# Opening of the attention stages with heads of 16: a second spare bank, three scores ahead, row statistics in pieces

## The chip, the cores and the metric

One core of one Trainium2 chip runs the whole program. The metric is device time in microseconds (us), the median of three runs; lower is better. TensorE (PE) multiplies matrices into eight PSUM banks, VectorE (DVE) and ScalarE (ACT) empty those banks, GpSimd (POOL) does elementwise work and issues some transfers, and SyncE (SP) issues the others.

## What is computed

Four layers on x (4 batches x 512 rows x 256 columns, float32), each an attention and then a feed-forward network on normalised rows, both added to x. The attentions of layers 0, 1 and 3 have 16 heads of 16; layer 2 has heads of 32 and is not touched by what follows. Cut to the first layer that matters:

```python
q = (x @ Wq + bq).reshape(B, LQ, 16, 16).transpose(0, 2, 1, 3)      # layer 1
k = (ctx @ Wk + bk).reshape(B, LKV, 16, 16).transpose(0, 2, 1, 3)
v = (ctx @ Wv + bv).reshape(B, LKV, 16, 16).transpose(0, 2, 1, 3)
attn = softmax(einsum('bhqd,bhkd->bhqk', q, k) * 0.25)
x = x + (einsum('bhqk,bhkd->bhqd', attn, v) ... ) @ Wo + bo
```

Layer 0 does this twice for each batch with the same input: causal self-attention over x and cross-attention over ctx. Layer 3 is like layer 1 without biases. x is passed through a layer norm ahead of each attention.

## The kernel before

`attention` (L429) runs one attention stage. Its work is cut into **units**: eight heads of one batch of one job. Layer 0 has 16 units (4 batches, 2 jobs, 2 halves of the heads), layers 1 and 3 have 8. Unit 0 and unit 1 share a batch; in layers 1 and 3 unit 2 is the first of batch 1, in layer 0 it is the cross-attention of batch 0.

A unit needs, in this order:

- its k and its q, each projected on PE into one spare bank (L2021), copied twice by ACT into a full and a rounded half (L2474, L2475; the second copy frees the bank), split by POOL into the low half (L2643), written to DRAM by SP (L2752, L2753), and read back as a **stack** (L2762) in tiles named KS and QS;
- 16 **maxima steps** (4 pairs of heads x 4 query tiles): two matmuls into a double bank `bank_t` (L2092, in layer 0's causal job also mask matmuls, L2030), and one DVE reduction that empties it (L2281). After the last one DVE makes the row maxima (L2291, L2293), PE turns them (L2117), and they go through DRAM into QS (L2766, L2773);
- 16 **logits steps**: two matmuls into a `bank_t` (L2104) and one exponential on ACT that empties it (L2488);
- after every second logits step, eight matmuls of the probabilities with V into `bank_o` (L2134). V is projected once for each batch and job in two pieces (L2021 from Wv, emptied by L2271 on DVE, or in layer 3 by L2479 on ACT).

There are three `bank_t`, handed out in turn to maxima steps and logits steps, so each step waits until the step three before it in that row has been emptied. `misc` is a ring of spare banks for all other PE work. It holds one bank, `bank_m`: each projection, turn or V piece waits until the one before it has been copied out.

What sets the order is a small planner in `attention`. One **tick** is one logits step. `feed` hands out maxima steps up to a limit, at most two in a tick. `chores` is a list of other steps; in the main loop one of them is taken every second tick (gap 2). A step is put in every engine's program at the same place, and each engine runs its program in order.

The **opening** of a stage with heads of 16 is the code from L816 on: project unit 0 and unit 1 while the 16 maxima steps of unit 0 run; then `feed(lead, lead)`, which adds the first six maxima steps of unit 1 (`lead` is 22); then `begun` (layer 0 alone: turn the context with `load_context`, in four groups, and wait for the weights); then V of unit 0, `norm.rest`, k and q of unit 2, all before the first logits step. `norm.rest` is the layer norm's statistics of all batches that have none yet (L2209 and L2213, one instruction each for every tile of 128 rows) and, behind them, twelve small instructions for the inverse root (L2218 to L2232, called `root`). In layer 3 unit 2's k and q stand behind the normalising of batch 1 (L2239) and its turn (L2042, L2244, L2457), and so behind those statistics. Then the main loop begins.

## Time and profile before

| | |
|---|---|
| median of 3 runs | 3419.75 us (3411.82 to 3423.57) |
| the profiled execution's own time | 3418.18 us |
| its span, first to last instruction | 3416.4 us |
| mean granted TensorE clock | 0.887 of 2.4 GHz |
| busy | PE 2794.7 us (82%), DVE 1979.2 (58%), ACT 1440.9 (42%), POOL 1142.7 (33%) |

The stages run one after the other, with a wait of all engines for all others between them. Layer 0's attention begins at 0, layer 1's at about 660 us and layer 3's at about 2889 us. The rows below are the PE and DVE rows of these three openings. In a timeline row the bracket at the end is the idle time just before the row and what ended it.

### The profile page before, as it was taken

Reading aid. Unit: us, or ns where it says so; the run is one execution under the profiler, and the core shown is the slowest. Engines: PE = TensorE matmul, PEld = TensorE weight load, DVE = VectorE, ACT = ScalarE, POOL = GpSimd, SP = SyncE. Lnnn points to the kernel's source line nnn. Section 1 sums busy time; section 2 is a strip of 40 time slices with the busy share of each in tenths; the row PEclk is TensorE's granted clock in tenths of the full one; section 3 lists DMA queues with packets and bytes.
Section 4 is the critical chain, followed back from the end, with each engine's and each line's share of the span. In section 5 each row is a group of like instructions: output and inputs, shape, how many; then the busy total and the mean of one; then the engine's idle time right before and its main releaser. Section 6 shows DMA issues by size and latency. Waiting matters only on the chain. (4 is left out here: it accounts for less than half of the span.)

```text
span 3416.4 us, 45781 instructions
## 1 busy us (share of the span) xinstructions
PE 2794.7 (82%) x17261; PEld 1597.9 (47%) x17268; DVE 1979.2 (58%) x3631; ACT 1440.9 (42%) x1932; POOL 1142.7 (33%) x1030
## 2 busy tenths in 40 slices
PE   5898887778879789999867899778999998688544
PEld 2343433623336444445743344367777777233222
DVE  3655666577646364445747656664354443577588
ACT  1456556246622244545214455333333432266423
POOL 2233332213232246655315778640010110222333
PEclk7889997879969999999987999799999998699766
DMA  5666561155410001112100000001211221565100
GB/s 143 120 122 128 124 144 34 31 101 125 96 47 1 16 25 44 43 40 75 31 13 1 1 1 1 26 1 29 97 56 48 64 65 50 99 121 103 34 11 15
DMA packets 129740, 198.58 MB, mean 58 GB/s; under 512 B 36272, under 2 KB 66480, under 8 KB 129392
## 3 DMA queue, kind: packets, MB, share of 16 engines
q1 hardware_dynamic: 97776, 143.23, 18.5%
q0 software_dynamic: 31744, 52.41, 5.8%
q8 instruction: 138, 2.26, 0.3%
q14 instruction: 82, 0.67, 0.1%
HBM read 130.73 MB, written 64.75 MB: 57 GB/s over the span
## 5 line engine op out<-in xcount | busy, mean ns | idle before, releaser
L2281 DVE TENSOR_REDUCE L_mx<-bank_t 128x2 f32<-128x1024 f32 (+3 forms) x512 | 565.9, 1122 | 353.1 <-PE bank_t L2092 223.8
L2281 DVE TENSOR_REDUCE L2a_mx<-bank_t 128x2 f32<-128x1024 f32 x256 | 311.2, 1222 | 392.5 <-PE bank_t L2069 391.5
L2488 ACT ACTIVATE L_P<-bank_t 128x1024 f32<-128x1024 f32 (+3 forms) x384 | 340.0, 916 | 248.7 <-PE bank_t L2104 138.1
L2488 ACT ACTIVATE L2a_P<-bank_t 128x1024 f32<-128x1024 f32 x256 | 261.9, 1024 | 285.1 <-PE bank_t L2081 284.8
L2092 PE MATMUL bank_t<-L_KS,L_QS 48*128 48x512 f32 (+2 forms) x1024 | 242.6, 475 | 122.6 <-ACT L_P L2488 50.0
L2069 PE MATMUL bank_t<-L2a_QK 32*128 32x512 f32 x1536 | 252.9, 447 | 71.7 <-ACT L2a_P L2488 28.5
L2104 PE MATMUL bank_t<-L_QS,L_KS 50*128 50x512 f32 (+2 forms) x1024 | 243.2, 478 | 23.4 <-DMA L_QS<-L_spill_max_rows 12.6
L2077 PE MATMUL bank_t<-L2a_QK 32*128 32x512 f32 x1536 | 257.2, 443 | 0.0
L2069 PEld LDWEIGHTS bank_t<-L2a_QK 32*128 32x128 f32 x1536 | 136.9, 197 | 234.3 <-ACT L2a_P L2488 111.6
L2104 PEld LDWEIGHTS bank_t<-L_QS,L_KS 50*128 50x128 f32 x1024 | 100.5, 196 | 258.4 <-issue 170.8
L2134 PE MATMUL bank_o<-L_P,L_V 128*32 128x512 f32 (+3 forms) x1536 | 201.1, 599 | 8.2 <-ACT L_P L2488 7.0
L2021 PE MATMUL bank_t<-L2g_act_high,L2g_w_high 128*128 128x512 f32 x472 | 187.3, 397 | 19.3 <-DVE L2g_w_low L2365 17.0
L2092 PEld LDWEIGHTS bank_t<-L_KS,L_QS 48*128 48x128 f32 x1024 | 107.7, 207 | 199.5 <-ACT L_P L2488 85.8
L2643 POOL TENSOR_TENSOR L_lo<-L_full,L_hi 128x512 fp32r<-128x512 f32 x64 | 81.5, 1273 | 346.6 <-ACT L_hi L2475 317.4
L2372 DVE TENSOR_TENSOR L2g_act_low<-ctxT,L2g_act_high 128x512 fp32r<-128x512 f32 x96 | 67.4, 703 | 223.2 <-ACT L2g_act_high L2529 223.2
L2021 PE MATMUL bank_t<-L2g_act_low,L2g_w_high 128*128 128x512 f32 x472 | 185.3, 393 | 0.0
L2021 PE MATMUL bank_t<-L2g_act_high,L2g_w_low 128*128 128x512 f32 x472 | 185.0, 392 | 0.0
L2653 POOL TENSOR_TENSOR L2a_sums<-L2a_sums,L2a_P 128x1024 f32<-128x1024 f32 x64 | 153.3, 2396 | 18.3 <-ACT L2a_P L2488 14.0
L2648 POOL TENSOR_TENSOR L2a_diag<-L2a_P,after_q 128x256 f32<-128x256 f32 x128 | 95.2, 744 | 144.9 <-issue 80.0
L2134 PE MATMUL bank_o<-L2a_P,L2a_V 128*32 128x512 f32 (+3 forms) x896 | 138.8, 555 | 1.7 <-ACT L2a_P L2488 1.7
L2138 PE MATMUL bank_o<-L2a_P,ones 128*32 128x512 f32 x512 | 137.6, 614 | 0.0
L2077 PEld LDWEIGHTS bank_t<-L2a_QK 32*128 32x128 f32 x1536 | 130.1, 193 | 14.4 <-issue 11.3
(444 smaller groups left out, 6184.8 us busy)
## 6 DMA issues: line engine op xcount, KB each, us to landing
L_KS<-L_spill_k_halves SPq DMA_DIRECT2D x174, 128.0 KB, 5.3
L_QS<-L_spill_q_halves SPq DMA_DIRECT2D x174, 128.0 KB, 4.6
L_spill_raw<-xn POOLq DMA_DIRECT2D x64, 256.0 KB, 2.5
L2g_raw<-in_L_ffn_h_blocks SPq DMA_DIRECT2D x32, 512.0 KB, 3.8
L_spill_k_halves<-L_hi SPq DMA_DIRECT2D x32, 256.0 KB, 2.1
L_spill_k_halves<-L_lo SPq DMA_DIRECT2D x32, 256.0 KB, 2.4
L_spill_q_halves<-L_hi SPq DMA_DIRECT2D x32, 256.0 KB, 2.2
L_spill_q_halves<-L_lo SPq DMA_DIRECT2D x32, 256.0 KB, 2.8
```

The lines of the kernel that those rows point to most:

```text
L2021: mm = e.matmul(out_, w, x, start=first and i == 0, stop=last and i == len(terms) - 1)
L2069: mm = e.matmul(m.tile[:, c, :], Q[r, m.qt * P:(m.qt + 1) * P], K[r, :], start=i == 0, stop=i == 2)
L2077: e.matmul(l.tile[:, c, :], K[r, l.kt * P:(l.kt + 1) * P], Q[r, :], start=i == 0, stop=False)
L2092: mm = e.matmul(m.tile[:, c, 0:n_keys], st.QS[m.un.buf][rows, slot, m.qt * P:(m.qt + 1) * P], st.KS[m.un.buf][rows, slot, 0:n_keys], start ...
L2104: mm = e.matmul(x.tile[:, c, q0:S], st.KS[x.un.buf][rows, slot, x.kt * P:(x.kt + 1) * P], st.QS[x.un.buf][rows, slot, q0:S], start=True, s ...
L2134: mm = e.matmul(bank_o[row:row + 32, q0:q1], V[:, s.kt, head, :], moving, start=s.first and i == 0, stop=s.last and i == len(cuts) - 1, ti ...
L2138: mm = e.matmul(bank_o[row + 32:row + 64, :], ones[:, 0:32], s.at.Pr[pb][:, c, :], start=s.first, stop=s.last, tile_position=(0, row + 32))
L2281: e.tensor_reduce(neg, s.tile[:, :, 0:n_keys], AX.X, ALU.max, negate=True).then_inc(sem(s.done), 1)
L2488: e.activation(s.at.Pr[s.pb][:, :, q0:S], s.tile[:, :, q0:S], ACT.Exp, scale=s.at.scale).then_inc(sem(s.exp), 1)
L2643: e.tensor_tensor(s.low[:, :], s.full, s.high[:, :].bitcast(F32), ALU.subtract).then_inc(sem(s.lo), 1)
L2648: e.tensor_tensor(s.dst[:, :, :], s.src, after_q[:, :].unsqueeze(1).to_broadcast([P, 2, P]), ALU.mult).then_inc(sem(s.done), 1)
L2653: e.tensor_tensor(s.dst[:, :, :], s.a[:, :, :], s.b[:, :, :], ALU.add).then_inc(sem(s.done), 1)
```

## The change

The diff is in full. It does four things, all in stages with heads of 16 except that `norm.rest()` now returns a list:

- `misc` has two banks, `bank_m` and `bank_o`, until unit 0's V and unit 2's k and q are projected. Then `bank_o` is taken out of the ring and goes to the values.
- Ahead of that point three maxima steps of unit 1 are fed, not six. The rest is fed in the loop, two in a tick until the old distance is reached.
- `begun` becomes a chore behind unit 1's projections, among the maxima steps of unit 0.
- `norm.rest()` gives one chore for each batch and one for the root. These come after the main loop has begun, in front of the projections of unit 3 (units[1]'s V is an empty list here).

```diff
--- before.py
+++ after.py
@@ -350,8 +350,14 @@
                 self.e_stats[b:b + 1 if b1 is None else b1] = [e] * (1 if b1 is None else b1 - b)
 
             def rest(self):
-                if None in self.e_stats:
-                    self.stats(self.e_stats.index(None), B)
+                if None not in self.e_stats:
+                    return []
+                b0 = self.e_stats.index(None)
+
+                def roots():
+                    self.e_stats[b0:B] = [root(TB * b0, TB * B)] * (B - b0)
+                return [lambda b=b: rows_stats(lambda t: X[:, t, :], self.loaded, TB * b, TB * b + TB)
+                        for b in range(b0, B)] + [roots]
 
             def steps(self, b, ring, more=(), later=lambda n, step: step()):
                 if self.ready[b] is not None:
@@ -470,8 +476,8 @@
 
             tiles = Banks([bank_t[i] for i in range(3)])
             tiles.free = [[ALL.free[2 * i], ALL.free[2 * i + 1]] for i in range(3)]
-            o_free, misc = [ALL.free[6]], Banks([bank_m[:, :]])
-            misc.free = [ALL.free[7]]
+            o_free, misc = [ALL.free[6]], Banks([bank_m[:, :], bank_o[:, :]][:2 if D == 16 else 1])
+            misc.free = [ALL.free[7], ALL.free[6]][:2 if D == 16 else 1]
 
             units = []
             for b in range(B):
@@ -818,9 +824,11 @@
             if D == 16:
                 add(StackRest(st, st.ready, st.v_ones))
                 chores += prepare(units[1])
+                if begun is not None:
+                    chores.append(lambda: begun(misc))
             else:
                 if norm is not None:
-                    chores.append(norm.rest)
+                    chores += norm.rest()
                 chores += value_steps(units[0])
                 for un in units[1:st.n]:
                     chores += prepare(un)
@@ -829,15 +837,17 @@
                 add_fed(feed(unit_ticks))
                 run_due(gapped=False)
             run_all()
-            add_fed(feed(lead, lead))
             if D == 16:
-                if begun is not None:
-                    begun(misc)
-                chores += value_steps(units[0])
+                add_fed(feed(unit_ticks + 3, 3))
+                chores += value_steps(units[0]) + prepare(units[2])
+                run_all()
+                o_free[0] = misc.free.pop()
+                misc.aps.pop()
                 if norm is not None:
-                    chores.append(norm.rest)
-                chores += prepare(units[2]) + value_steps(units[1])
-                run_all()
+                    chores += norm.rest()
+                chores += value_steps(units[1])
+            else:
+                add_fed(feed(lead, lead))
             if side is not None:
                 side.ring, side.busy = misc, hi_free
                 chores += side.rest()
```

**PE, layer 0, from unit 1's maxima steps (out of KS, QS) to the first logits step (out of QS, KS).** Before:

```order
L2092 MATMUL bank_t<-L_KS,L_QS 128x128 x2
L2030 MATMUL bank_t<-L_mask_steps,L_mask_pick 128x64 x4
L2092 MATMUL bank_t<-L_KS,L_QS 128x256 x2
L2030 MATMUL bank_t<-L_mask_steps,L_mask_pick 128x64 x4
L2042 MATMUL bank_m<-ident,xn 128x128 x16
L2021 MATMUL bank_m<-L_Wv,XT 128x256 x8
L2021 MATMUL bank_m<-ctxT,L_Wck 128x512
L2021 MATMUL bank_m<-XT,L_Wcq 128x512 x2
L2092 MATMUL bank_t<-L_KS,L_QS 128x384 x2
L2030 MATMUL bank_t<-L_mask_steps,L_mask_pick 128x64 x4
L2104 MATMUL bank_t<-L_QS,L_KS 128x512 x2
```

With the change:

```order
L2102 MATMUL bank_t<-L_KS,L_QS 128x384 x2
L2040 MATMUL bank_t<-L_mask_steps,L_mask_pick 128x64 x4
L2031 MATMUL bank_o<-L_Wv,XT 128x256 x4
L2031 MATMUL bank_m<-L_Wv,XT 128x256 x4
L2031 MATMUL bank_o<-ctxT,L_Wck 128x512
L2031 MATMUL bank_m<-XT,L_Wcq 128x512 x2
L2102 MATMUL bank_t<-L_KS,L_QS 128x512 x2
L2040 MATMUL bank_t<-L_mask_steps,L_mask_pick 128x64 x4
L2102 MATMUL bank_t<-L_KS,L_QS 128x128 x2
L2040 MATMUL bank_t<-L_mask_steps,L_mask_pick 128x64 x4
L2114 MATMUL bank_t<-L_QS,L_KS 128x512 x2
```

The context's 16 turns are gone from here (they stand in four groups behind unit 0's sixth maxima step), three maxima steps have moved behind the projections of V, k (Wck) and q (Wcq), and two banks take turns. The line numbers of the change are ten higher.

**DVE, layer 1, from unit 1's first maxima steps on.** With the change:

```order
L2291 TENSOR_REDUCE L_mx<-bank_t 128x2 x3
L2281 TENSOR_TENSOR L_V<-bank_o,L_bv 128x32x16
L2281 TENSOR_TENSOR L_V<-bank_m,L_bv 128x32x16
L2291 TENSOR_REDUCE L_mx<-bank_t 128x2 x4
L2219 BN_STATS stats<-X 128x6 x4
L2223 BN_AGGR mv<-stats 128x2 x4
L2291 TENSOR_REDUCE L_mx<-bank_t 128x2 x3
L2219 BN_STATS stats<-X 128x6 x4
L2223 BN_AGGR mv<-stats 128x2 x4
L2291 TENSOR_REDUCE L_mx<-bank_t 128x2 x2
L2228 TENSOR_SCALAR nw<-mv 128x8
...
L2291 TENSOR_REDUCE L_mx<-bank_t 128x2 x4
```

Before, the same place reads:

```order
L2281 TENSOR_REDUCE L_mx<-bank_t 128x2 x6
L2271 TENSOR_TENSOR L_V<-bank_m,L_bv 128x32x16 x2
L2209 BN_STATS stats<-X 128x6 x8
L2213 BN_AGGR mv<-stats 128x2 x8
L2218 TENSOR_SCALAR nw<-mv 128x8
...
L2232 SCALAR_TENSOR_TENSOR rstd<-nw 128x8
L2281 TENSOR_REDUCE L_mx<-bank_t 128x2 x10
```

The eight tiles' statistics and the root stood between the V pieces and the loop's first reduction; now they stand in three pieces between the loop's first nine reductions.

**DVE, layer 3, the same place with the change, up to unit 2's normalised rows and their turn:**

```order
L2291 TENSOR_REDUCE L_mx<-bank_t 128x2 x3
L2219 BN_STATS stats<-X 128x6 x4
L2223 BN_AGGR mv<-stats 128x2 x4
L2228 TENSOR_SCALAR nw<-mv 128x4
...
L2242 SCALAR_TENSOR_TENSOR rstd<-nw 128x4
L2249 TENSOR_SCALAR xn<-X,mv,rstd 128x256 x4
L2254 COPY XT<-bank_m 128x512
L2291 TENSOR_REDUCE L_mx<-bank_t 128x2 x4
L2219 BN_STATS stats<-X 128x6 x4
L2223 BN_AGGR mv<-stats 128x2 x4
```

The statistics of four tiles stand ahead of the normalising, where twelve stood, and three reductions ahead of them, where six stood. Behind the first two units of each of the three stages the order is again the same on every engine.

## Rows read from the trace of the kernel before

**Rows 1.** Stretches of layer 0, busy us by engine; first line names the columns.
```profile
core 0: us, PE busy (x) PEld busy (x) DVE busy (x) ACT busy (x) POOL busy (x), PEclk, DMA share, GB/s
85.00:102.40 17.40, 16.31 (x107) 7.14 (x108) 6.57 (x13) 7.07 (x10) 2.54 (x2) 0.60 0.86 138
```

**Rows 2.** Timeline of PE, layer 0: start, duration, engine, line, tiles, count, idle before.
```profile
58.94 0.47 PE L2092 MATMUL bank_t<-L_KS,L_QS 48*128 48x128 f32 x2 [5.46 <-DMA L_QS<-L_spill_q_halves]
...
67.76 1.12 PE L2042 MATMUL bank_m<-ident,xn 128*128 128x128 f32 x4 [0.69 <-ACT ctxT L2457]
69.66 3.75 PE L2021 MATMUL bank_m<-L_Wv,XT 128*128 128x256 f32 x8 [0.78 <-ACT ctxT L2457]
74.39 3.78 PE L2021 MATMUL bank_m<-L_Wv,XT 128*128 128x256 f32 x8 [0.98 <-DVE L_V L2271]
78.95 1.13 PE L2021 MATMUL bank_m<-ctxT,L_Wck 128*128 128x512 f32 x2 [0.78 <-DVE L_V L2271]
81.59 3.45 PE L2021 MATMUL bank_m<-XT,L_Wcq 128*128 128x512 f32 x4 [1.51 <-ACT L_hi L2475]
84.97 0.62 PE L2092 MATMUL bank_t<-L_KS,L_QS 48*128 48x384 f32 x2
...
102.43 0.36 PE L2092 MATMUL bank_t<-L_KS,L_QS 48*128 48x256 f32 x2
```

**Rows 3.** Timeline of PE, layer 1.
```profile
662.80 3.38 PE L2021 MATMUL bank_m<-XT,L_Wq 128*128 128x512 f32 x4 [1.44 <-ACT L_hi L2475]
...
703.65 1.65 PE L2092 MATMUL bank_t<-L_KS,L_QS 48*128 48x512 f32 x6 [2.18 <-DMA L_QS<-L_spill_q_halves]
...
708.75 2.07 PE L2021 MATMUL bank_m<-L_Wv,ctxT 128*128 128x256 f32 x4
...
718.31 3.78 PE L2021 MATMUL bank_m<-XT,L_Wq 128*128 128x512 f32 x4 [1.36 <-ACT L_hi L2475]
722.02 0.80 PE L2092 MATMUL bank_t<-L_KS,L_QS 48*128 48x512 f32 x2
...
737.68 1.98 PE L2021 MATMUL bank_m<-XT,L_Wq 128*128 128x512 f32 x4
...
742.38 1.13 PE L2021 MATMUL bank_m<-L_Wv,ctxT 128*128 128x256 f32 x4 [0.37 <-ACT L_hi L2475]
```

**Rows 4.** Timeline of PE, layer 3.
```profile
2941.42 1.65 PE L2092 MATMUL bank_t<-L_KS,L_QS 48*128 48x512 f32 x6 [0.30 <-DMA L_QS<-L_spill_q_halves]
...
2957.93 1.11 PE L2042 MATMUL bank_m<-ident,xn 128*128 128x128 f32 x4 [6.58 <-DVE xn L2239]
...
2968.77 0.80 PE L2092 MATMUL bank_t<-L_KS,L_QS 48*128 48x512 f32 x2
```

**Rows 5.** Timeline of DVE, layers 0 and 1.
```profile
42.92 9.03 DVE L2281 TENSOR_REDUCE L_mx<-bank_t 128x2 f32<-128x256 f32 x12 [2.36 <-PE bank_t L2030]
...
704.49 6.88 DVE L2281 TENSOR_REDUCE L_mx<-bank_t 128x2 f32<-128x1024 f32 x6 [4.09 <-PE bank_t L2092]
...
714.74 2.70 DVE L2209 BATCH_NORM_STATS2 stats<-X 128x6 f32<-128x256 f32 x8
717.47 0.64 DVE L2213 BATCH_NORM_AGGREGATE mv<-stats 128x2 f32<-128x6 f32 x8
...
718.56 1.21 DVE L2223 TENSOR_SCALAR nw<-nw 128x8 f32<-128x8 f32 x1
...
735.03 1.23 DVE L2281 TENSOR_REDUCE L_mx<-bank_t 128x2 f32<-128x1024 f32 x1 [1.93 <-PE bank_t L2092]
```

**Rows 6.** Timeline of DVE, layer 3.
```profile
2953.09 0.91 DVE L2213 BATCH_NORM_AGGREGATE mv<-stats 128x2 f32<-128x6 f32 x12
...
2956.49 1.38 DVE L2239 TENSOR_SCALAR xn<-X,mv,rstd 128x256 f32<-128x256 f32 x4
...
2981.02 1.23 DVE L2281 TENSOR_REDUCE L_mx<-bank_t 128x2 f32<-128x1024 f32 x1 [1.15 <-PE bank_t L2092]
```

**Rows 7.** Timeline of POOL, layer 1.
```profile
718.47 1.27 POOL L2643 TENSOR_TENSOR L_lo<-L_full,L_hi 128x512 fp32r<-128x512 f32 x1 [30.34 <-ACT L_hi L2475]
```

## The prediction

> **What bounds the kernel now.** I read the table of stretches, then the PE and DVE timelines of the three openings of stages with heads of 16. "t" is a tick of the main loop, t0 its first; S is a maxima step.
>
> In the openings the bound is a chain of PE steps, each waiting until the one spare bank is emptied. Layer 0: PE waits 5.46 us for unit 1's stack until 58.94; then come six S, four turns of the context with 0.69 us of idle between them, two V pieces of 3.75 and 3.78 us, k and q (idle 0.78 to 1.51 us before each), and the loop begins at 84.97 [rows 2]. Layer 1 is the same without context: 703.65 to 722.02 [rows 3]. In layer 3 PE also waits 6.58 us for normalised rows that stand behind the statistics of twelve tiles: 2941.42 to 2968.77 [rows 4]. In the loop that follows PE is nearly full (16.31 of 17.40 us) and DVE is not (6.57) [rows 1]. So time saved ahead of the loop counts only as far as the loop's first ticks don't take it back.
>
> **The change, part by part.** Sum for each opening: when does the loop begin, and what do its first ticks cost.
>
> *Two banks ahead of the stack.* q no longer waits for k's copies. In layer 1 that wait is 1.44 us [rows 3], and q's spill, read and first S follow q; layer 3 is built alike. I let unit 1's stack land 1.4 us earlier in both: 702.2 and 2940.0. It can be nothing, if the reads are held by the transfer queue and not by their start; both ends stay in the range. In layer 0 I count nothing here (58.94).
>
> *Layer 0, to t0.* The turns of the context go among unit 0's S. There they cost four times 1.12 us of PE at most [rows 2] and delay the reductions; the slack is the 5.46 us for which PE waits for the stack anyway, so nothing is left on the path. From 58.94: three S 1.75 us (half the six, 3.4 us, rounded up), V 3.75 + 3.78 = 7.53 without a wait, k 1.13 to 2.08, q 3.45 to 3.78 [rows 2, 3] (k has half of q's matmuls, so the slow price of k is about half of 3.78 and a little over). t0 at 58.94 + 1.75 + 7.53 + 1.4 + 3.6 = 73.2, against 84.97: 11.8 us earlier.
>
> *Layer 1, to t0.* 702.2 + three S 1.65 + V 2 x 2.07 + k 2.0 + q 3.78 [rows 3] = 713.8. DVE is done with three reductions of 1.15 us (6.88 for six [rows 5]) and a V piece before k wants its bank. Against 722.02: 8.2 us.
>
> *Layer 3, to t0.* From 2940.0: 0.8 us to the first reduction, three reductions 3.45 us, four tiles' statistics 1.67 us (half of 2.70 + 0.64 [rows 5]), root 2.49 us (2954.00 to 2956.49 [rows 6]), normalising 1.38 us [rows 6]: 2949.8. Two turns of 1.11 us without a wait between, k 2.0, q 3.78 as in layer 1 [rows 3, 4]: 2957.8, against 2968.77: 11.0 us. The two V pieces fit in PE's wait.
>
> *The first ticks.* Here the change pays back. Three S and all statistics now stand between the loop's first reductions. Layers 1 and 3: up to the end of the reduction of t6's S, DVE has ten reductions (11.5 us), two statistics pieces (3.34 us) and a root (2.49 us); with 0.8 us until the first can start and some 0.9 us of waits that is 19.0 us, and DVE is what PE waits for through the `bank_t`. Before, it was 735.03 + 1.23 - 722.02 = 14.2 us in layer 1 and 2981.02 + 1.23 - 2968.77 = 13.5 us in layer 3 [rows 3 to 6]. So 4.8 and 5.5 us are given back, and k of unit 3, which moves from t4 to t6, runs in PE's waits. Net: 8.2 - 4.8 = 3.4 us and 11.0 - 5.5 = 5.5 us. Layer 0 has shorter causal reductions, 0.75 us (9.03 for twelve [rows 5]). Ten of them 7.5 us, three pieces 5.0, root 2.5: 15.0 us on DVE up to t7, and on PE about 12.6 us (16.31 us of [rows 1] less 3.78 and 2.08 for q and k makes 10.5 for 14 steps and the values; three more steps, 2 us). So about 15 us, then k and q of unit 3, which before stood inside, 3.1 to 5.9 us. Together 19.7 us against 102.43 - 84.97 = 17.5 [rows 2]: 2.3 us given back. Net 9.5 us.
>
> *Clock of TensorE.* All V, k and q pieces here but one ran at the 1.2 GHz level: 3.78 us for q where the same shape took 1.98 at 2.4 GHz, 2.07 for V where it took 1.13 [rows 3]. In layer 0 the level rose right behind the V piece that ran 74.39 to 78.17 (k then took 1.13 us) and was low again for q after 1.51 us of idle [rows 2]. With two banks these pieces run without a gap, so it may rise earlier. If it does: 3.4 us of V in layer 0, 1.8 us for q in layers 1 and 3, 7.0 us in all. If not: 0. I take 2.0, nearer to nothing, since layer 1's q at 718.31 was slow although V and k had run just before it.
> The Trainium skill, "TensorE: Matmul & The Clock Gate", section Part 1, says that the low level is the default and sustained activity releases it. By that rule the 7.0 us would come in full, and the total would be 25.4 us; the trace agrees for the one case in layer 0, and layer 1's q, behind 1.36 us of idle, neither shows nor excludes it.
>
> *Stalls of DVE beside POOL.* One root step took 1.21 us, where twelve of them took 2.49 in layer 3 [rows 6], while POOL's 1.27 us split ran from 718.47 [rows 5, 7]. Such a stall was beside PE work until now; in the loop it would be on the path. 0 to 1.0 us for each opening, 3 in all; I take 0, since one root in three met it.
> The Trainium skill, "SBUF — State Buffer", section "SBUF: two separate sides", says that the two engines share a port pair held by one instruction at a time, the loser being blocked fully. By it each root that meets a split pays that 1.0 us; this rule speaks against moving the root into the loop. The row agrees.
>
> **Sum.** 9.5 + 3.4 + 5.5 + 2.0 = 20.4 us. The profiled execution took 3418.18 us, 1.6 under the median of the three: 3397.8.
>
> **Rivals.**
> *A, as summed:* 3397.8; with its own bounds (stack no earlier -2.8, stalls -3, layer 0's k and q at the low level -1.5; clock up to +5.0) 3392 to 3406.
> *B, the first ticks take nearly all back.* DVE and PE wait for each other in turn: two S in one tick need two `bank_t` of three, and each piece of statistics then holds PE twice. If what is left in layers 1 and 3 (3.4 + 5.5 us) is lost outright, the clock gives nothing and layer 0 keeps 6 us, the gain is 6: 3412. For it: DVE's load is above PE's in those ticks. Against: only six or seven ticks long, and the PE work moved there fills the waits.
> *C, the clock rises in each opening* and stays up in the first ticks: 18.4 + 7.0, and some 1.3 us more in each loop: 29 us, 3389. For it: [rows 2] at 78.95. Against: [rows 3] at 718.31.
> *D, slower: the clock is lost.* PE waits for DVE in the first ticks, falls to 1.2 GHz and stays there. Price: a tick with values costs about 0.5 us more at that level (q alone 1.8 more). It decides from 40 such ticks on; if units 0 and 1 of all three stages (96 ticks) ran so, +48 - 20: 3446; 60 ticks: 3428. Against it: at 737.68 the level is high again about nine ticks into layer 1's loop although the ticks before it had waits.
> *E, no gain ahead of the loop:* unit 1's stack or maxima rows land later than PE is ready, because the context's turns delay unit 0's maxima in layer 0: 3.4 + 5.5 are left, without a gain by the clock: 3409.
>
> **Chances.** A 0.54, B 0.19, C 0.16, D 0.05, E 0.06. The range takes in C and B's nearer part: 3387 to 3411. A difference under 0.3% (10.3 us, from 3409.5) can't be told from none by this measurement. Faster than that: A, C and half of E and a little of B, 0.76; within: most of B, rest of E, 0.19; slower: D, 0.05.
>
> **What would show it.** In the trace after: q of unit 0 in layers 1 and 3 without a wait before it; the first logits about 11.8, 8.2 and 11 us sooner after the stage's start; in layer 3 the wait before the turn down from 6.58 to about 4 us. Then in the six ticks behind it PE waiting for DVE's reductions, DVE without gaps, and the tick t7 only 9.5, 3.4 and 5.5 us sooner. Wrong if the granted clock of the openings differs much, if PE still waits for a spare bank before k or q, or if anything behind the first two units of a stage changes its length by more than a few us.

## The result: 3382.48 us, 0.990 of before, and below the forecast's range

The changed kernel takes 3382.48 us (median of 6 runs, 3372.96 to 3397.53) against 3417.09 us for the kernel before (6 runs of the same comparison). The ratio is 0.990, 95% interval 0.9877 to 0.9922. The forecast was 3397.8 with a range from 3387 to 3411: the sign was right, the size was not. The profiled execution of the change took 3381.53 us, 36.6 less than the profiled execution of before, where 20.4 had been summed. Medians and ratios in this document are of undisturbed executions: one each of e5 and e12 and two of before, 4% to 83% longer than the rest, are left out.

The table of stretches of both kernels, each opening taken from a stage's first k projection to t0; before first, then the change (the first line names the columns):

```profile
core 0: us, PE busy (x) PEld busy (x) DVE busy (x) ACT busy (x) POOL busy (x), PEclk, DMA share, GB/s
13.97:84.97 71.00, 40.56 (x191) 21.87 (x191) 23.86 (x56) 9.31 (x15) 15.36 (x11) 0.64 0.52 118
660.27:722.02 61.75, 35.37 (x74) 13.47 (x75) 36.75 (x56) 6.92 (x11) 15.37 (x11) 0.57 0.48 94
2898.22:2968.77 70.55, 38.38 (x82) 14.86 (x82) 34.59 (x65) 8.71 (x14) 15.36 (x11) 0.55 0.40 83
```

```profile
14.10:70.45 56.35, 33.11 (x172) 18.73 (x173) 15.98 (x23) 9.09 (x15) 14.29 (x11) 0.73 0.67 142
648.69:696.80 48.11, 27.86 (x69) 11.81 (x70) 27.06 (x25) 6.91 (x11) 14.22 (x11) 0.65 0.59 111
2868.14:2924.65 56.51, 31.12 (x77) 14.01 (x78) 27.97 (x46) 8.71 (x14) 14.65 (x11) 0.63 0.47 95
```

The openings are 14.7, 13.6 and 14.0 us shorter; forecast were 11.8, 8.2 and 11.0. The granted clock in them is 0.63 to 0.73, where it was 0.55 to 0.64. Three maxima steps fewer stand ahead of t0, so a part must be given back.

PE of the change in layer 0, V, k and q of unit 2 and t0; the rows of before are [rows 2]:

```profile
61.80 3.78 PE L2031 MATMUL bank_o<-L_Wv,XT 128*128 128x256 f32 x8
65.38 2.38 PE L2031 MATMUL bank_m<-L_Wv,XT 128*128 128x256 f32 x8
67.59 1.02 PE L2031 MATMUL bank_o<-ctxT,L_Wck 128*128 128x512 f32 x2
68.54 1.98 PE L2031 MATMUL bank_m<-XT,L_Wcq 128*128 128x512 f32 x4
70.45 0.50 PE L2102 MATMUL bank_t<-L_KS,L_QS 48*128 48x512 f32 x2
```

PE in layer 1, from unit 0's q to the first ticks; before [rows 3]:

```profile
649.63 1.88 PE L2031 MATMUL bank_o<-XT,L_Wq 128*128 128x512 f32 x4
...
688.69 1.65 PE L2102 MATMUL bank_t<-L_KS,L_QS 48*128 48x512 f32 x6 [1.97 <-DMA L_QS<-L_spill_q_halves]
690.27 2.07 PE L2031 MATMUL bank_o<-L_Wv,ctxT 128*128 128x256 f32 x4
692.13 1.91 PE L2031 MATMUL bank_m<-L_Wv,ctxT 128*128 128x256 f32 x4
693.84 1.31 PE L2031 MATMUL bank_o<-ctxT,L_Wk 128*128 128x512 f32 x2
694.99 1.88 PE L2031 MATMUL bank_m<-XT,L_Wq 128*128 128x512 f32 x4
696.80 0.74 PE L2102 MATMUL bank_t<-L_KS,L_QS 48*128 48x512 f32 x4
...
698.63 0.50 PE L2102 MATMUL bank_t<-L_KS,L_QS 48*128 48x512 f32 x2 [0.86 <-DVE L_mx L2291]
...
704.85 0.79 PE L2102 MATMUL bank_t<-L_KS,L_QS 48*128 48x512 f32 x2 [1.61 <-DVE L_mx L2291]
```

From 688.69 to 696.80 the only bracket is the one in front of the first row: PE waits for nothing. V and k become shorter, and q takes 1.88 us where it took 3.78 (k, with half of q's matmuls, takes 1.31 where it took 2.08). In layer 3 PE waits 5.01 us for the normalised rows (6.58 before [rows 4]), and q takes 2.36:

```profile
2918.69 1.11 PE L2052 MATMUL bank_o<-ident,xn 128*128 128x128 f32 x4 [5.01 <-DVE xn L2249]
...
2922.36 2.36 PE L2031 MATMUL bank_m<-XT,L_Wq 128*128 128x512 f32 x4
2924.65 0.74 PE L2102 MATMUL bank_t<-L_KS,L_QS 48*128 48x512 f32 x4
```

DVE of the change in the first ticks of layer 1; before [rows 5]. It has hardly a gap from 697.35 until the root is done at 713.8, and PE waits for it (0.86 and 1.61 above):

```profile
697.35 4.62 DVE L2291 TENSOR_REDUCE L_mx<-bank_t 128x2 f32<-128x1024 f32 x4 [2.57 <-PE bank_t L2102]
701.88 1.40 DVE L2219 BATCH_NORM_STATS2 stats<-X 128x6 f32<-128x256 f32 x4
...
703.61 3.45 DVE L2291 TENSOR_REDUCE L_mx<-bank_t 128x2 f32<-128x1024 f32 x3
...
711.40 0.16 DVE L2228 TENSOR_SCALAR nw<-mv 128x8 f32<-128x8 f32 x1
...
713.70 2.35 DVE L2291 TENSOR_REDUCE L_mx<-bank_t 128x2 f32<-128x1024 f32 x2
```

### The profile page after: what moved, and what is told of

The parts are those of the page before. It is cut to its first block and busy times, and to the rows that moved or that the text cites. A ratio compares the mean times of both kernels' runs of the same rounds, so it can differ in the third digit from the quotient of the medians.

```text
span 3379.8 us, 45802 instructions
## 1 busy us (share of the span) xinstructions
PE 2767.3 (82%) x17268; PEld 1589.2 (47%) x17268; DVE 1978.0 (59%) x3643; ACT 1440.1 (43%) x1932; POOL 1143.1 (34%) x1030
## 5 line engine op out<-in xcount | busy, mean ns | idle before, releaser
L2114 PE MATMUL bank_t<-L_QS,L_KS 50*128 50x512 f32 (+2 forms) x1024 | 243.0, 478 | 21.4 <-DVE L_mx L2291 10.8
```

The costliest lines, as they stand in the source:

```text
L2114: mm = e.matmul(x.tile[:, c, q0:S], st.KS[x.un.buf][rows, slot, x.kt * P:(x.kt + 1) * P], st.QS[x.un.buf][rows, slot, q0:S], start=True, s ...
```

## The experiments

Two readings are taken from each trace, and stand in the table beside the median. **t0** is the start of the loop, counted in us from the stage's first k projection. **Kept** is what is left once the first ticks have given back their part: each ACT instruction is matched with the same one of the profiled kernel before, both are counted from the stage's first k, and the differences are averaged 130 to 160 us on in layers 1 and 3 and 200 to 300 us on in layer 0; a negative number is time saved. The second execution of before (e13) shows how far kept is to be trusted: within some 1.5 us in layers 0 and 3, and 4 us in layer 1. The three executions of the change differ by up to 3.6 us.

| kernel | median us | ratio (95% interval) | t0 in layers 0, 1, 3 | kept in layers 0, 1, 3 |
|---|---|---|---|---|
| before (profiled) | 3417.1 | | 71.0, 61.8, 70.6 | |
| change | 3382.5 | 0.9900 (0.9877 to 0.9922) | 56.4, 48.1, 56.5 | -15.0, -9.3, -8.6 |
| e8 change again | 3377.7 | 0.9910 (0.9888 to 0.9932) | 57.0, 46.5, 56.1 | -12.8, -8.0, -9.6 |
| e18 change, third time | 3383.1 | 0.9894 (0.9867 to 0.9921) | 55.8, 46.5, 56.5 | -15.6, -11.6, -9.1 |
| e13 before again | 3412.6 | 1.0006 (0.9989 to 1.0022) | 71.7, 59.8, 71.0 | +1.1, -4.0, +1.4 |
| e1 change, one bank | 3405.2 | 0.9979 (0.9956 to 1.0003) | 58.3, 58.5, 64.7 | -10.2, +3.8, -3.8 |
| e16 the same, waits filled | 3415.5 | 1.0001 (0.9980 to 1.0022) | 60.2, 55.4, 63.2 | -10.0, +1.7, -1.9 |
| e7 change, second bank late | 3392.6 | 0.9937 (0.9915 to 0.9960) | 58.3, 52.0, 60.1 | -13.6, -1.8, -9.1 |
| e5 before, second bank only | 3386.2 | 0.9938 (0.9910 to 0.9967) | 58.1, 49.8, 62.8 | -10.0, -11.1, -11.0 |
| e6 before, waits filled | 3416.0 | 1.0024 (1.0002 to 1.0047) | 69.6, 59.1, 68.6 | -6.6, +1.0, -6.5 |
| e3 change, statistics in front | 3384.6 | 0.9916 (0.9887 to 0.9945) | 56.9, 46.7, 59.1 | -6.0, -11.1, -10.2 |
| e11 before, statistics in pieces | 3414.4 | 0.9998 (0.9979 to 1.0018) | 72.1, 61.9, 67.8 | -4.4, +3.7, -4.0 |
| e4 change, context back | 3376.5 | 0.9893 (0.9867 to 0.9920) | 58.5, 46.6, 58.0 | -15.0, -10.8, -10.5 |
| e2 change, six ahead | 3373.7 | 0.9894 (0.9857 to 0.9932) | 56.3, 51.5, 59.1 | -21.3, -7.7, -10.9 |
| e9 change, six and context back | 3384.9 | 0.9914 (0.9880 to 0.9948) | 58.6, 50.4, 59.5 | -17.9, -10.4, -9.6 |
| e10 change, none ahead | 3372.1 | 0.9879 (0.9846 to 0.9912) | 50.6, 45.3, 49.6 | -17.8, -10.2, -14.2 |
| e17 the same again | 3373.4 | 0.9869 (0.9842 to 0.9897) | 49.4, 45.0, 48.9 | -14.9, -10.3, -13.7 |
| e14 none ahead, statistics behind k and q | 3373.4 | 0.9888 (0.9867 to 0.9908) | 50.1, 45.2, 48.6 | -16.5, -9.5, -14.1 |
| e12 change, idle work in a wait | 3374.5 | 0.9882 (0.9852 to 0.9912) | 52.8, 46.9, 55.6 | -19.6, -7.5, -13.3 |
| e15 e14 with idle work | 3377.4 | 0.9899 (0.9874 to 0.9924) | 52.2, 43.2, 50.2 | -12.1, -10.6, -16.8 |

Each ratio is against the runs of before in its own comparison (medians 3410 to 3417).

### The second bank

The change with one spare bank:

```diff
-            o_free, misc = [ALL.free[6]], Banks([bank_m[:, :], bank_o[:, :]][:2 if D == 16 else 1])
-            misc.free = [ALL.free[7], ALL.free[6]][:2 if D == 16 else 1]
+            o_free, misc = [ALL.free[6]], Banks([bank_m[:, :]])
+            misc.free = [ALL.free[7]]
...
-                o_free[0] = misc.free.pop()
-                misc.aps.pop()
```

> The changed kernel with one spare bank all the time; its other parts stay. Counted from a stage's first k projection, the loop begins 56.4, 48.1 and 56.5 us later with the change (layers 0, 1, 3). Theory 1, the second bank works through TensorE's clock: without it the waits of 0.8 to 1.5 us come back before each V piece, k and q, and the engine is at the low level again in them, so V, k and q of unit 2 take 3.8, 2.1 and 3.8 us in place of 1.9 to 2.4, about 1.3 and 1.9 to 2.4. Then the loop begins 6 to 8 us later in each opening and the kernel takes about 3382 + 20 = 3402. Rival, only the waits count: the same waits come back, 3 to 4 us an opening, but the pieces keep their lengths: 3393.

3405.2 us. PE in layer 1 of this kernel:

```profile
694.70 2.07 PE L2029 MATMUL bank_m<-L_Wv,ctxT 128*128 128x256 f32 x4
698.09 2.07 PE L2029 MATMUL bank_m<-L_Wv,ctxT 128*128 128x256 f32 x4 [1.32 <-DVE L_V L2279]
700.95 2.08 PE L2029 MATMUL bank_m<-ctxT,L_Wk 128*128 128x512 f32 x2 [0.79 <-DVE L_V L2279]
704.38 3.78 PE L2029 MATMUL bank_m<-XT,L_Wq 128*128 128x512 f32 x4 [1.35 <-ACT L_hi L2483]
708.09 1.22 PE L2100 MATMUL bank_t<-L_KS,L_QS 48*128 48x512 f32 x4
```

The waits are back, and with them the lengths of [rows 3]: theory 1 for layers 1 and 3 (10.4 and 8.1 us later). In layer 0 the loop begins only 1.9 us later, because k and q keep 1.12 and 1.98 us there although they wait: behind V pieces of 3.78 and 1.99 us the level stayed high across waits of 0.78 and 1.36 us. In the kernel before it did not (q 3.45 us behind a wait of 1.51 [rows 2]), so this is one case and not a rule. In layer 1 nothing of the gain is left, within the 4 us of that reading: with one bank, the other three parts show no gain there.

To part wait and level, the same kernel was given idle work in those waits (matmuls into `bank_o`, which nothing else uses then; their definition is left out):

```diff
-                chores += value_steps(units[0]) + prepare(units[2])
+                steps = prepare(units[2])
+                chores += filled(value_steps(units[0]), [0, 2]) + steps[:-2] + filled(steps[-2:], [2, 3])
```

> The changed kernel with one spare bank, and idle matmuls in TensorE's waits for that bank: two of 128x256 ahead of the second V piece and of unit 2's k, three ahead of its q. Theory 1 (of the 10.4 and 8.1 us by which one bank delays the loop in layers 1 and 3, the pieces' level is 3 to 4 us, the waits in them and in front the rest): q takes 1.98 in place of 3.78, the loop begins 2.5 to 4 us sooner than with one bank unfilled, at 54.5 to 56 and 61 to 62 us. Rival (the level is a small part): less than 1.5 us sooner.

PE in layer 1; the rows into bank_o are the idle work:

```profile
704.33 2.07 PE L2039 MATMUL bank_m<-L_Wv,ctxT 128*128 128x256 f32 x4
706.20 1.91 PE L2060 MATMUL bank_o<-XT,ident 128*128 128x256 f32 x4
707.90 1.60 PE L2039 MATMUL bank_m<-L_Wv,ctxT 128*128 128x256 f32 x4
709.34 1.03 PE L2060 MATMUL bank_o<-XT,ident 128*128 128x256 f32 x4
710.29 1.13 PE L2039 MATMUL bank_m<-ctxT,L_Wk 128*128 128x512 f32 x2
711.25 1.46 PE L2060 MATMUL bank_o<-XT,ident 128*128 128x256 f32 x6
712.77 1.98 PE L2039 MATMUL bank_m<-XT,L_Wq 128*128 128x512 f32 x4
```

The bank's waits are still there, filled, and k takes 1.13 and q 1.98 us. From the first V to t0 the granted clock reads (one bank, one bank filled, then the change):

```profile
694.70:708.09 13.39, 9.93 (x16) 4.01 (x15) 4.03 (x5) 1.26 (x2) 1.26 (x1) 0.50 0.11 40
704.33:714.68 10.35, 10.29 (x30) 6.59 (x28) 4.03 (x5) 1.27 (x2) 1.26 (x1) 0.77 0.00 0
690.27:696.80 6.53, 6.53 (x17) 3.77 (x16) 4.03 (x5) 1.26 (x2) 0.13 (x1) 0.68 0.01 3
```

So in this place it is work without gaps that brings the high level, not the bank as such. Layer 1 takes 13.4 us there with one bank, 10.4 with one bank filled and 6.5 with two: 3.0 us are the level's, 3.8 the waits'. In layer 3 the filling is worth 1.5 us, less than expected, and in layer 0, where the level was high already, it costs 0.7 from V to t0 (the other 1.3 us arose ahead of V). The median, though, is 3415.5, 10 us above the unfilled kernel's, and the two ratios' intervals overlap; kept is 2.1 us better in layer 1 and 1.9 worse in layer 3. So the level's part is shown at t0, and that it stays by itself is not. Nearly the same filling (one matmul less ahead of k) in the kernel before:

> The kernel before, one spare bank, with idle TensorE work added in its waits: two matmuls of 128x256 into the unused accumulator bank ahead of the second V piece, one ahead of unit 2's k, three ahead of its q. Nothing else changes. Theory 1 (the level follows from work without gaps): q of unit 2 takes 1.98 in place of 3.78 us in layers 1 and 3, V and k get shorter too, and the loop begins 1 to 3 us sooner in each opening although PE has more to do. Rival (it was the banks' handing on alone, and the level in these pieces is chance): q stays at 3.78, and the loop begins 0 to 1 us later.

q takes 1.98 us in all three openings, and the loop begins 1.4, 2.6 and 2.0 us sooner (2.2, 0.7 and 2.4 against e13). Theory 1 holds for the openings, and the kernel is still 0.2% slower (1.0002 to 1.0047). The traces show where, but not why. e6 kept 6.6 us in layer 0 and yet comes to layer 1's first k 4.7 us later than before; e16 kept 10.0 and is 1.2 ahead there, e1 kept 10.2 and is 10.8 ahead. Between 500 and 550 us, where the order of the instructions is the same again, the granted clock was 0.67 in e6 and 0.68 in e16, against 0.71 in e1 and 0.76 and 0.90 in the two executions of before. But e3, which has no idle work, shows it too (0.67, from 6.0 ahead to 1.6 behind), and the three executions of the change are 11.7, 21.7 and 16.3 us ahead at that k. That idle work is the cause is not shown.

The bank alone, added to the kernel before:

> The kernel before with the second spare bank alone: six maxima steps ahead of the loop, context and statistics where they were. Theory 1 (the bank is most of the gain, directly and through TensorE's clock): the loop begins 6 to 8 us sooner in layer 0, 9 to 10 in layer 1 (3.4 of it because q of unit 0 follows k at once and at the high level), 4 to 6 in layer 3, where the statistics still stand ahead; what is left 100 us on is 4, 9 and 3 us at least, the time about 3392 to 3396. Rival (the parts work only together, since with six steps ahead DVE is late and PE waits for it): less than 5 us in all, 3407.

3386.2: 21 us under before by the ratio (11 to 31 by its interval), where the change has 33; the loop begins 12.9, 12.0 and 7.8 us sooner, more than expected. The rival falls. By kept it holds 32.1 us in its three openings, as much as the change's 32.9: these traces don't show what the other three parts add, the medians alone do, within their spread. And the change with the bank given only for V, k and q of unit 2:

> The changed kernel with the second bank given only behind unit 1's first three maxima steps, for V, k and q of unit 2; units 0 and 1 are projected through one bank. Theory 1 (the front's gain is q of unit 0 behind k, 1.5 us of wait and 1.5 us of clock): unit 1's stack comes 3.4 us later in layer 1, 2.5 in layer 3 and about 0 in layer 0 than with the change, V, k and q keep their short times, and the kernel takes 3382 + 6 = 3388. Rival (stack and reads are held by the queue, the front gives nothing): the loop begins at the same place, 3382.

Unit 0's q takes 3.5 us again in layer 1, behind 1.4 us of wait, and the loop begins 3.9 us later than in the change (5.5 than in e8), in layer 3 3.6 and in layer 0 about 1.6. The median is 15 us above e8's and 10 above the change's: at least the 6 expected. The front is a part of its own.

### The other three parts

Statistics and root ahead of the loop again:

```diff
-                chores += value_steps(units[0]) + prepare(units[2])
+                chores += value_steps(units[0]) + (norm.rest() if norm is not None else []) + prepare(units[2])
```

> The changed kernel with the other batches' statistics and root ahead of unit 2's normalising again, that is ahead of the loop. Theory 1 (DVE's work is only moved, and DVE is what the first ticks wait for): layer 0 and 1 begin the loop at the same place and are within 1 us 100 us on; layer 3 begins it 3 to 4 us later (eight more tiles of statistics, 3.3 us, before the rows are normalised) and gets back most of it: 3384. Rival (statistics in the first ticks cost nothing, ahead of the loop everything): 3382 + 3.3 = 3386, and all 3.3 us of layer 3 stay.

Wrong in layer 0 by both theories. The loop begins at the same place, and then PE waits 5.65 us, since DVE works off twelve tiles' statistics and the root before it empties the `bank_t` of the steps at t0:

```profile
77.88 0.58 PE L2100 MATMUL bank_t<-L_KS,L_QS 48*128 48x256 f32 x2 [5.65 <-DVE L_mx L2289]
```

Kept in layer 0 is 6.0 us, against 12.8 to 15.6 with pieces. This is one trace, the slowest of four executions; the median, 3384.6, is not apart from the change's. In layers 1 and 3 the pieces are worth nothing (kept 11.1 and 10.2 us with statistics in front). In the kernel before the pieces alone bring nothing:

> The kernel before with the statistics in pieces behind the first logits steps alone: one spare bank, six ahead, context where it was. Theory 1 (TensorE waits for the bank and not for DVE as long as there is one bank, so the statistics lay beside that wait in layers 0 and 1; in layer 3 they stood ahead of the turn): the loop begins at the same place in layers 0 and 1 and 3 to 4 us sooner in layer 3, most of it given back: 3406 to 3410 against 3410. Rival (the 8.7 us that layer 0 lost with the statistics back in front are lost in the kernel before as well): 3400, layer 0 alone 7 to 9 us sooner 200 us on.

Theory 1 holds (0.9998); layer 0's 4.4 us are matched by a slower layer 1. By these traces the pieces pay only in layer 0 and only once the second bank has brought the loop forward.

The context behind unit 1's first maxima steps again, and the same with six ahead (`feed(lead, lead)`):

> The changed kernel with the four turns of the context behind unit 1's first three maxima steps again, as before the change; layer 0 alone. Theory 1: four times 1.12 us of TensorE at the low level come back between the maxima steps and V, with two banks hiding the copies, so layer 0's loop begins 4.5 us later; the clock has then risen by the V pieces (3.8 + 2.1), which gives 1 to 1.5 us back: +3 to +3.5, 3385. Rival: the turns' waits for their copies (0.7 us each) come back as well: +7, 3389.

> The changed kernel with six maxima steps of unit 1 ahead of the loop, as before the change, in place of three. Theory 1 (three steps moved into the loop cost there about what they save ahead of it in layers 1 and 3): the loop begins 1.7 to 3.5 us later in each opening, DVE's queue in the first ticks is 3.5 us shorter, and 100 us on nothing is left of the difference: 3382, within 3. Rival (the first ticks had room for the three steps): all of it stays, 3382 + 3 x 2.5 = 3390.

> The changed kernel with both six maxima steps ahead and the context behind them, so what is left of the change is the second bank and the statistics in pieces. Theory 1 (these two parts are the whole gain, the other two are worth less than 3 us each): 3376 to 3382, as the change, 0.990 of before. Rival A (each of the two undone parts was a loss, since the kernels without one of them took 3374 and 3376): their gains add, 3368 to 3372. Rival B (three ahead and the context among unit 0's steps do carry a part): 3386 or more, layer 0's loop beginning 6 us later and staying so.

Layer 0's loop begins 1.5 to 2.7 us later with the context back (e4 against the change's three executions), less than expected. With six ahead it begins 3.4 and 2.6 us later in layers 1 and 3, and nothing of that stays: kept is about the same in layers 1 and 3. In layer 0, where t0 does not move, it is larger (21.3, and 17.9 in e9, against 12.8 to 15.6), which these runs don't explain. The medians of the first two, 3376.5 and 3373.7, are not above the change's; both undone together give 3384.9. Their gains do not add (rival A falls), and 10 us between such medians can't be told from chance here. By e9, bank and pieces alone carry about 29 of the 33 us (18 to 41 by its interval).

None ahead (the line `add_fed(feed(unit_ticks + 3, 3))` taken out), twice:

> The changed kernel with none of unit 1's maxima steps ahead of the loop in place of three. Theory 1 (TensorE and DVE owe the same steps on either side of the loop's beginning): the loop begins 1.3 to 1.7 us sooner in each opening and all of it is given back in the first ticks, with 0 to 2 us more since DVE is what they wait for: 3382 to 3386. Rival (steps in the first ticks are free): 1.5 us more gain in each opening, 3377.

> The changed kernel with none of unit 1's maxima steps ahead of the loop, once more, beside the change in the same call. Theory 1 (what its openings hold more, 3 us in layer 0 and 5 to 6 in layer 3, is real, since in layer 3 the statistics, the normalising and the turn of unit 2 wait for three reductions less): 5 to 9 us below the change, 3372 to 3375, 200 us on again 3 us more in layer 0 and 5 us more in layer 3. Rival (its first time was a good draw): within 3 us of the change.

In layer 1 the loop begins 1.2 to 3.2 us sooner and nothing of it stays: given back in full, as theory 1 of the first run says. In layer 0 it begins some 6 us sooner; the 3 us more that the first run kept are not seen in the second. In layer 3 it begins 7 us sooner and 4 to 5 stay both times, which the first run's expectation missed. Here is PE in layer 3 of e17:

```profile
2917.72 0.66 PE L2051 MATMUL bank_o<-ident,xn 128*128 128x128 f32 x4 [1.10 <-DVE xn L2248]
...
2921.84 0.73 PE L2101 MATMUL bank_t<-L_KS,L_QS 48*128 48x512 f32 x4
```

The wait for the normalised rows is 1.10 us, where it was 5.01: the three reductions (3.49 us) stood ahead of the statistics on DVE. The medians are 3372.1 and 3373.4, and in the shared comparison 0.9869 against 0.9894 for the change (3383.1). The intervals overlap; that both medians lie some 10 us under the change's middle one speaks for none ahead, of which 4 to 5 us are seen in layer 3. No version had a lower median, but e2 and e14 (3373.7 and 3373.4) are not apart from it.

The remaining statistics right behind unit 2's projections, in layers 1 and 3, to empty DVE's queue for the first ticks (in layer 3 this kernel works out batch 1's statistics twice):

> The changed kernel with no maxima step of unit 1 ahead of the loop and, in layers 1 and 3, the remaining statistics and the root right behind the projections of unit 2 and ahead of the loop, where DVE would be idle; layer 0 keeps its pieces in the loop. Theory 1 (what the first ticks give back is DVE's queue): TensorE begins the loop at the same time as with none ahead (45.3 and 49.6 us), the first ticks have 5.8 us less DVE work in layer 1 and layer 3, and 2 to 4 us more are left in each: 3372 - 5 = 3367. Rival (the first ticks are bound by TensorE's own work, or DVE comes late to the first reduction): nothing gained, 3372 to 3376.

The rival: 3373.4. DVE then starts its first reduction only at 694.31 in layer 1, 4.4 us behind t0 at 689.91, and works through ten in a row. Moving DVE's work from one side of t0 to the other shifts the wait.

### Idle work in the long wait

> The changed kernel with 16 idle matmuls of 128x512 on TensorE while it waits for unit 0's stack (11 to 14 us of wait), into the next spare bank. Theory 1 (the level follows what TensorE has just done, so work in the wait keeps it high through unit 1's k and q): k of unit 1 takes about 1.1 in place of 2.07 us and q 1.98 in place of 2.2 to 3.8, its stack comes 1 to 3 us sooner in layers 1 and 3, the loop too: 3382 - 4 = 3378. Rival A (idle work costs its gain elsewhere, as where the gaps were filled): the openings gain that, the total does not move, 3382. Rival B (at the low level the 16 take 16 us and run past the stack's arrival): the loop begins 2 to 5 us later in each opening, 3392.

> The same with the 16 idle matmuls of 128x512 in TensorE's wait for unit 0's stack. Theory 1 (the level kept high through unit 1's k and q adds its 1 to 1.5 us in layers 0 and 1): 1 to 4 us below the kernel without them, 3364. Rival (in layers 1 and 3 they run past the stack's arrival by 2.8 to 3.4 us and take back what they give): the same time.

PE in layer 1 of e12, unit 1's k and q:

```profile
657.76 1.12 PE L2039 MATMUL bank_m<-ctxT,L_Wk 128*128 128x512 f32 x2
...
659.48 1.98 PE L2039 MATMUL bank_o<-XT,L_Wq 128*128 128x512 f32 x4
```

They took 2.07 and 2.5 to 3.8 us in the change. But the idle work runs past the arrival of unit 0's stack, taken from the change's trace, by 2.8 us in layer 1 and 3.4 in layer 3, so that t0 moves by 1.2 us at most there; in layer 0 it comes 3.0 to 4.2 us sooner. The medians, 3374.5 and 3377.4, are not apart from the same kernels without idle work.

### Both kernels again

> The changed kernel once more. Theory 1: what the openings gain is the same in each execution, within 1 us in each (the loop begins 56.4, 48.1 and 56.5 us behind the stage's first k), and the difference elsewhere, such as 10 us in the later part of layer 1, is the clock's and goes another way in another execution by some 5 us. Rival: the 10 us in layer 1's later part are a lasting effect of the change and are seen again.

> The kernel before once more, profiled. Theory 1 (its profiled execution of 3418 was a long one of its kind, and what all kernels seemed to gain 160 to 200 us into layer 1 was its loss alone): the new profiled execution takes 3405 to 3412, layer 1 comes out of the stretch 155 to 200 us behind its first k 3 to 4 us sooner, and the openings are the same within 1 us. Rival (the profile of before was typical): 3418 again, the same stretch as long as it was.

> The changed kernel a third time, as the other side of the comparison with none ahead. Theory 1: 3378 to 3383 and 0.990 to 0.991 of before, and the loop begins 56 to 57, 46.5 to 48.5 and 56 to 57 us behind the first k of layers 0, 1 and 3. Rival: 3372 to 3376, so that its first two medians were slow draws.

The openings repeat within 1.7 us at t0 for the change and 1.9 for before, not within 1: in layer 1 unit 1's q took 3.78 us in the first execution of the change and 2.5 in the other two. In that first execution PE works without a gap from 662.40, and the level is still low 8 us on, so unbroken work alone does not say when it rises:

```profile
662.40:670.49 8.09, 8.09 (x14) 2.67 (x14) 4.71 (x4) 1.26 (x2) 2.49 (x2) 0.50 1.04 171
```

The change's medians are 3382.5, 3377.7 and 3383.1, always 32 to 35 us under before. The new profiled execution of before took 3411.5 us, 6.7 less than the first, and differs most in layer 1: q of unit 0 took 1.98 in place of 3.38 us, and the stretch in which all kernels seemed to gain reads (first execution, then second):

```profile
809.00:821.00 12.00, 10.06 (x44) 4.45 (x42) 8.39 (x10) 5.27 (x6) 4.35 (x4) 0.72 0.87 129
```

```profile
809.00:821.00 12.00, 10.59 (x66) 4.60 (x63) 10.63 (x14) 7.34 (x9) 4.83 (x4) 1.00 0.88 132
```

At 0.72 of the clock the first does 44 matmuls, at 1.00 the second does 66. These 3 us belong to one execution of before and not to the change. The 10 us that the change gained beyond kept by 600 us into layer 1 came back as about 8 and 7 in its other two executions. The second execution of before is itself 5 to 6 us ahead of the first there, 3 of them in this stretch, so about half belongs to the first execution of before; the remainder is not explained by these runs.

## Why the forecast was wrong, step by step

The miss is 15.3 us. The openings kept 15.0 + 9.3 + 8.6 = 32.9 us against 20.4 summed, clock term included: 12.5. The profiled executions differ by another 3.7 elsewhere. That is a net figure: 3.3 are lost again in layer 0 behind kept, 9.2 more are gained between the first k of layer 1 and that of layer 3, some 3 of them in the stretch just shown, in which the execution that the sum started from was slow, and 2.1 are lost in layer 3. Against the second execution of before the openings kept 16.1, 5.3 and 10.0, in all 31.4, so the sum is firm and layer 1's share is not. The change's median lies 0.9 above its profiled execution, which takes that much off.

- **Two banks ahead of the stack, 1.4 us: too small.** Unit 1's stack is there 43.4 us behind the first k before (703.65) and 40.0 after (688.69), 3.4 sooner in layer 1 and 2.5 in layer 3. The wait of 1.44 was counted; that q behind k at once also runs at the high level (1.88 for 3.38 us) was not. e7 confirms it. In layer 0 the stack came 1.1 us later, where nothing was counted.
- **V, k and q up to t0, and the clock's 2.0 us: the step that failed.** From the first V to t0, 12.5 us were summed in layer 0 and 8.65 measured, 9.9 and 6.5 in layer 1, and from k on 5.8 and 4.2 in layer 3. That is 8.9 us for the three, and with the front's q 10 to 11, where 2.0 were taken and 7.0 were the upper bound. The 2.0 was chosen from layer 1's slow q at 718.31, which stood behind a wait; in e16 and e6, with the wait filled, the same q took 1.98. These lengths are measured up to t0; that they stay is shown only together with the waits' part (kept). Two rows of before spoke against reading the level from one piece and the wait in front of it: high behind 1.51 us of wait, low behind 0.20.

```profile
19.00 1.98 PE L2021 MATMUL bank_m<-XT,L_Wq 128*128 128x512 f32 x4 [1.51 <-ACT L_hi L2475]
...
681.56 3.78 PE L2021 MATMUL bank_m<-XT,L_Wq 128*128 128x512 f32 x4 [0.20 <-ACT L_hi L2475]
```

  The Trainium skill ("TensorE: Matmul & The Clock Gate", section Part 1) says that the low level is the default and activity releases it; by that rule the forecast had named 7.0 and 25.4 in all. The traces agree for unit 2's V, k and q (q 1.88 to 2.38 us in all three openings of all three executions), not for unit 1's q in layer 1, 3.78 us after 4.3 us of work without a gap. Rival C had the rise right and was still short; its high level did not last through the first ticks (the logits step at t0 took 0.40 us, the third 0.63).
- **Layer 3's chain on DVE: right.** 9.8 us from stack to normalised rows were summed, 9.9 measured; PE's wait is 5.01, near the 4 foretold.
- **The first ticks: right in layer 3, about right in layer 1, too high in layer 0.** Given back are 13.6 - 9.3 = 4.3 and 14.0 - 8.6 = 5.4 us, against 4.8 and 5.5. Against the second execution of before it is 6.4 and 4.4, so layer 1's agreement is in part luck. Layer 0 gives back nothing, against 2.3; why is open. Rival B falls.
- **Stalls of DVE beside POOL, taken at 0: right.** No root step in the change's openings took over 0.17 us. Where e14 put a root beside POOL's split, one took 1.24:

```profile
691.55 1.24 DVE L2237 TENSOR_TENSOR nw<-nw 128x8 f32<-128x8 f32 x1
```

```profile
691.50 1.26 POOL L2654 TENSOR_TENSOR L_lo<-L_full,L_hi 128x512 fp32r<-128x512 f32 x1 [0.43 <-ACT L_hi L2486]
```

  The first row is DVE, the second POOL of the same kernel. The price was right; among these rows it is paid only where the two meet.
- **The place of layer 0's statistics.** The forecast saw it only as a load moved onto the first ticks. e3 shows that in front it would have cost 5.65 us of wait: with the loop's beginning forward, the statistics no longer lie beside PE's wait for the bank.
- **Rival D** did not occur, and E neither. A's own bounds add up to 3393 to 3405 and not to 3392 to 3406; nothing rests on it.

## What to carry to other kernels

Where a chain of TensorE pieces waits for a bank between them, price the second bank twice: the waits, and the pieces behind them at the length of the high level, since both go together (3.8 and 3.0 us up to t0 in one opening here). When a start is brought forward, look again at what used to stand beside the old wait on the emptying engine; it is now on the path. Steps moved across the start of a loop are worth what the engine with the longer queue saves, which was nothing in layer 1 and 4 to 5 us in layer 3, where a chain stood behind them.

## What the runs showed of the hardware

- A wait of 1.35 to 1.44 us did not settle the level: q behind it took 1.98 us in the second execution of before (layer 1, unit 0) and 3.38 in the first, and in e1 3.78 behind layer 1's short V pieces against 1.98 behind layer 0's long ones. Nor did work without a gap: 8.09 us of it ran at 0.50 in layer 1 of the change.
- Idle work on TensorE raised the level wherever the pieces behind it had run low (q of unit 2 1.88 to 1.98 us in e6 and e16), and the whole program gained nothing from it (1.0024 and 1.0001 for two kernels whose openings began their loops sooner in two or three stages).
- POOL's split stretched the one root step that met it (1.24 us for 0.17, e14). Statistics beside such a split (689.78 to 691.06 in e14) kept 1.38 us for four, and the change's four reductions out of PSUM at 697.35 beside the split at 698.39 took 4.62, 1.15 each as elsewhere.
- The same program's profiled executions differ in single stretches by the granted clock, 0.72 against 1.00 over 12 us; a difference of 3 us seen in one trace alone is not a result.
